# A two-layer early-fusion model on one core: image tokens built in two halves, and routed pages of 64 rows worked in pairs

## The chip, the core and the metric

The kernel runs on one core of one Trainium2 chip. The metric is the device time of one execution in microseconds (us). Before the change the median of three runs is 2499.37 us, with a lowest of 2489.65 and a highest of 2499.59. Everything is computed in float32.

## The reference

One function takes 128 images of 224 x 224, 32 text tokens of 64 numbers for each image, and the weights of two layers.

```
h = haar_tokens(x) @ W + b            # 7 wavelet maps, each resized to 8 x 8: 64 tokens of 64
h = concat([h, txt], axis=1)          # [128, 96, 64]: 64 image tokens, 32 text tokens
h = h + attention(layernorm(h))       # layer 0: gated attention, squared relu, rope
h = h + ffn(layernorm(h))             # layer 0: heads with 4 experts each
h = h + rwkv(layernorm(h))            # layer 1: the recurrence over 96 tokens, and its own ffn
h = h + moe(layernorm(h))             # layer 1: the part that the change touches most

def moe(x):                           # x: 128 * 96 = 12288 rows of 64
    logits = x @ Wr + br              # 64 experts
    top, idx = top_k(logits, 2);  gates = softmax(top)
    for e in range(64):
        y = relu(x @ W1[e] + b1[e]) @ W2[e] + b2[e]     # 64 -> 128 -> 64
        out += gate_of(e) * y
```

Each of the 12288 rows goes to two experts, so 24576 routed rows are computed.

## The kernel before

Each engine has one program, and semaphores join them. A helper, `grouped` (line 73), writes a software pipeline: it takes stages with a lag each, steps through iterations, and in step t calls each stage for iteration t minus its lag. So the order of the work on an engine is written by hand, as the order of the stages and their lags. `wait(engine, semaphore, n)` is a wait that is left out or trivial for the first iterations. An engine executes its program strictly in order; a wait holds up all that stands behind it on that engine.

*Tokenizer.* The 128 images are loaded in 32 groups (`NG`) of four by SyncE (`load_images`, line 419), through four buffers; the load of group g waits until TensorE has done group g - 4. For each group TensorE multiplies with the row filters (`image_rows`, 8 matmuls, line 476) and turns the result (`image_turn`, 2 transposes, line 484). ScalarE copies both out of PSUM (`keep_rows`, line 983, and `keep_turn`, line 990). Only when all 32 groups are done follow, once: the column products in two halves of 512 columns (line 495), two products for tables (lines 499 and 501; VectorE makes from them the selection matrices `gsel` and the rope tables, lines 1457 to 1472), the token products for each of the 8 token columns (line 509, 512 columns wide), copied with their bias by ScalarE (line 1000), and 16 turning steps of four transposes (line 518), which ScalarE copies into `H` (line 1004). SyncE loads the text rows after the images (line 424) and then writes zeros over `XD`, the DRAM buffer of routed rows, in 16 DMAs (line 430).

*The middle.* The attention, the first ffn, the recurrence and its ffn run from 144 to about 1740 us. The change leaves them alone.

*Routing.* 16 rounds (`NR`) of 8 batches. TensorE turns the normalized rows and computes the logits (`d_transpose`, `d_logits`), VectorE picks the best two experts and, with TensorE's counting products (`d_ranks`), a slot for each routed row (`d_places`, lines 1906 to 1946). The rows of an expert fill blocks of `SLOT` = 128 rows in `XD`, and a new block is opened where the last one is full; there are at most `NBLK` = 2 x 12288 / 128 + 64 = 256 blocks. `over` (line 1912) counts how many new blocks an expert opens in a round (at most 7), `tab1`/`tab2` (lines 1932 and 1933) mark which expert owns which block. GpSimd takes a power for the norm (`d_power`, line 1416), makes a label (line 1420) and scatters the rows by 12 indirect DMAs per round (`d_scatter`, line 1431), each row with its destination and its gate behind it (`ROW` = 66). At the end the table of the blocks' experts becomes `blku`, 256 words that ScalarE can read into a register (line 1955).

*Expert loop.* 64 iterations of `EB` = 4 blocks, 512 rows. For an iteration
- SyncE loads 4 blocks (`load_blocks`, line 437), one DMA, up to eight iterations ahead, waiting for `e_out` of eight iterations before;
- ScalarE picks the weights (`pick_weights`, lines 1301 and 1302): for each block it reads the expert's number from `blku` into a register (`value_load`) and copies 256 columns (W1 with its bias as a 65th row, W2, and b2) from `wall`, which holds all experts, into `wx`, a ring of four iterations that lies over `XR`;
- TensorE turns the rows (`e_transpose`, line 954), ScalarE copies them out (`e_rows`, line 1060) under a row of ones that two `memset` instructions have set (lines 1959 and 1960);
- TensorE computes the hidden values, 65 rows deep (`e_hidden`, line 963), VectorE takes the relu out of PSUM (`e_relu`, line 1965);
- TensorE computes the outputs (`e_output`, line 971), VectorE copies the destinations, adds b2 and multiplies by the gate (`e_out`, lines 1970, 1973, 1975);
- GpSimd stores the four blocks by four indirect DMAs to `YD` (`e_back`, line 1444), waiting for the stores of two iterations before.

After the loop SyncE loads `YD` back, two rows for each token, and VectorE adds them to `h`.

## Time and profile before

| what | value |
|---|---|
| runs shown, median (lowest to highest) | 2499.37 us (2489.65 to 2499.59) |
| the profiled execution: its own time | 2492.8 us |
| its span, first to last instruction | 2490.7 us |
| mean granted TensorE clock, share of full | 0.788 |
| busy: TensorE / VectorE / ScalarE / GpSimd | 1874.9 / 1614.3 / 1086.9 / 1086.6 us |
| chain that ended last, by engine | TensorE 31%, VectorE 23%, issue 18%, GpSimd 10%, unknown queue 9% |

A profile is one execution. PE is TensorE's matmul side, PEld its weight loads, DVE VectorE, ACT ScalarE, POOL GpSimd and SP SyncE. A busy time is the sum over an engine's instructions and says nothing of who waits for whom; for that one looks at what ended the idle time ahead of an instruction (the releaser). Register, branch, semaphore and DMA-issuing instructions aren't counted as busy, so an engine can be at work on them in a stretch that is shown as idle and named "issue". "remote" is written where the profile finds no releaser among the core's engines. Records of fp32 matmuls are several for each matmul of the program (x16 for the 8 of a group), so counts in the rows are records.

### The profile page before, as it was taken

The numbers are of one execution on the slowest core, as the hardware profiler recorded it, in microseconds if no ns is written. First come the engines' busy times: TensorE is split into PE (matmuls) and PEld (weight loads), VectorE is DVE, ScalarE is ACT, GpSimd is POOL, SyncE is SP. The second block draws the span as 40 slices with busy tenths as digits, with TensorE's granted clock in tenths as the row PEclk, the third lists the DMA queues.
The fourth block names the chain that finished last, engine by engine and source line by source line (L and its number), as shares of the span: only waits on it lengthen the run. The fifth ranks groups of instructions, "written<-read, shape, count | busy, mean of one in ns | idle before, by whom it ended". The sixth has DMA issues, their size and how long they took to land.

```text
span 2490.7 us, 52044 instructions
## 1 busy us (share of the span) xinstructions
PE 1874.9 (75%) x16279; PEld 1455.7 (58%) x16279; DVE 1614.3 (65%) x5056; ACT 1086.9 (44%) x3422; POOL 1086.6 (44%) x878
## 2 busy tenths in 40 slices
PE   5788887999999999999997477764333346766672
PEld 2257676777777777777775255553222236655562
DVE  0047773588888888888886699995888832222223
ACT  2277772344444444444443389883222123333330
POOL 0036660134434344434343322221888755655553
PEclk9989996899999999999997578796555555555555
DMA  9910000000000000000000000005100031111114
GB/s 283 287 58 0 0 0 1 1 2 2 2 0 0 0 0 0 0 0 0 0 0 1 0 1 1 1 0 172 37 23 22 23 94 41 42 39 37 40 35 164
DMA packets 85142, 87.76 MB, mean 35 GB/s; under 512 B 58560, under 2 KB 73024, under 8 KB 83776
## 3 DMA queue, kind: packets, MB, share of 16 engines
q1 hardware_dynamic: 70576, 68.63, 9.8%
q0 software_dynamic: 14336, 14.91, 1.8%
q10 hardware_dynamic: 144, 3.15, 0.3%
q8 instruction: 46, 0.75, 0.1%
q14 instruction: 40, 0.33, 0.0%
HBM read 56.82 MB, written 29.82 MB: 35 GB/s over the span
## 4 chain that ended last, share of the span: by engine, by line
PE 31%; DVE 23%; issue 18%; POOL 10%; another core or an unknown queue 9%; ACT 2%; DMA 1%; DVEq 1%; POOLq 0%; ACTq 0%; SPq 0%
POOL routed_rows L1431 5%; PE PS L674 5%; PE PS L641 3%; PE PS L708 3%; PE PS L689 3%; PE PS L971 2%; POOL rstd L1332 2%; DVE XR L1585 2%; DVE XR L1785 2%; DVE XR L1581 1%; PE PS L723 1%; PE PS L748 1%; DVE arena L1965 1%; PE PS L570 1%
## 5 line engine op out<-in xcount | busy, mean ns | idle before, releaser
L1444 POOL DMA_INDIRECT expert_rows<-arena x256 | 245.7, 960 | 193.2 <-DVE arena L1975 127.8
L1060 ACT ACTIVATE arena<-PS 128x384 f32<-128x384 f32 (+4 forms) x384 | 179.8, 486 | 306.1 <-remote 95.5
L1965 DVE TENSOR_SCALAR arena<-PS 128x512 f32<-128x512 f32 x64 | 44.3, 691 | 341.8 <-remote 216.4
L1581 DVE TENSOR_REDUCE XR<-PS 128x2 f32<-128x192 f32 (+2 forms) x768 | 173.8, 280 | 104.7 <-PE PS L674 104.7
L1431 POOL DMA_INDIRECT routed_rows<-XR,SLu x192 | 201.3, 1048 | 75.5 <-issue 70.4
L674 PE MATMUL PS<-arena 32*128 32x96 f32 (+2 forms) x3072 | 234.2, 285 | 0.0
L971 PE MATMUL PS<-XR,arena 128*128 128x64 f32 x512 | 126.0, 428 | 130.3 <-DVE arena L1965 130.2
L674 PEld LDWEIGHTS PS<-arena 32*128 32x128 f32 x3072 | 198.4, 192 | 20.6
L971 PEld LDWEIGHTS PS<-XR,arena 128*128 128x128 f32 x512 | 114.0, 328 | 157.2 <-DVE arena L1965 139.8
L1377 POOL TENSOR_TENSOR arena<-arena,mhalf 96x16 f32<-96x16 f32 x32 | 93.3, 2916 | 241.5 <-DVE arena L1627 241.5
L1096 ACT ACTIVATE XR<-PS 128x256 f32<-128x256 f32 x512 | 167.3, 380 | 67.1 <-PE PS L689 66.9
L1302 ACT ACTIVATE XR<-arena 128x256 f32 x256 | 106.6, 416 | 179.2 <-issue 113.4
L1060 ACT ACTIVATE XR<-PS 128x384 f32<-128x384 f32 (+1 forms) x160 | 83.5, 522 | 222.0 <-PE PS L708 167.6
L1585 DVE TENSOR_TENSOR XR<-PS,XR 128x192 f32<-128x192 f32 (+2 forms) x768 | 172.4, 278 | 0.0
L641 PE MATMUL PS<-arena,WP 128*128 128x192 f32 x640 | 151.4, 361 | 18.4 <-ACT arena L1060 17.9
L689 PE MATMUL PS<-WP,XR 128*128 128x128 f32 (+1 forms) x1024 | 163.6, 284 | 0.9 <-ACT XR L1096 0.9
L708 PE MATMUL PS<-XR,arena 96*32 96x128 f32 (+2 forms) x3072 | 148.7, 288 | 6.6 <-DVE arena L1600 5.0
L1367 POOL TENSOR_TENSOR XR<-arena 96x1024 f32<-96x1024 f32 x32 | 61.8, 1931 | 191.6 <-DVE arena L1617 191.6
L1332 POOL TENSOR_TENSOR rstd<-stat,mhalf 96x4 f32<-96x4 f32 x32 | 78.4, 2450 | 129.5 <-DVE stat L1492 129.5
L963 PE MATMUL PS<-arena,XR 65*128 65x128 f32 x512 | 129.4, 434 | 0.0
L641 PEld LDWEIGHTS PS<-arena,WP 128*128 128x128 f32 x640 | 105.5, 199 | 34.8 <-ACT arena L1060 19.7
L1351 POOL TENSOR_TENSOR rstd<-stat,mhalf 96x4 f32<-96x4 f32 x32 | 36.2, 1131 | 197.9 <-DVE stat L1554 184.3
(307 smaller groups left out, 4750.3 us busy)
## 6 DMA issues: line engine op xcount, KB each, us to landing
arena<-in_x_dram SPq DMA_DIRECT2D x32, 784.0 KB, 9.8
routed_rows<-zt SPq DMA_DIRECT2D x16, 528.0 KB, 6.0
arena<-routed_rows SPq DMA_DIRECT2D x64, 132.0 KB
arena<-in_t_experts_dram SPq DMA_DIRECT2D x8, 1024.0 KB, 12.5
expert_rows<-arena POOLq DMA_INDIRECT x256
WP<-in_t_pack_dram SPq DMA_DIRECT2D x1, 3425.0 KB, 20.3
mixed_rows<-Hb SPq DMA_DIRECT2D x4, 768.0 KB
routed_rows<-XR,SLu POOLq DMA_INDIRECT x192
```

The source lines that it names most:

```text
L641: mm = pe.matmul(o, w[:, par, :], sxF[:, u, :].rearrange("p (q t) -> p q t", q=2), start=True, stop=True)
L674: mm = pe.matmul(PS[:, S_ + i, S_AT[j]:S_AT[j] + QB * (j + 1)], qF[rows, u, 3 * b + j, :], kF[rows, u, keys], start=False, stop=True, skip ...
L689: mm = pe.transpose(PS[0:keys, T0_ + i, n * P:(n + 1) * P], Pe[:, p, i, n * P:n * P + keys], ident[:, :])
L708: mm = pe.matmul(PS[32 * n:32 * n + 32, O_, j * P:(j + 1) * P], Vx[rows, u, b * NH + n, :], PT[rows, b % 2, n, at:at + P], start=True, sto ...
L963: mm = pe.matmul(PS[:, 2 + u % 2, k * SLOT:(k + 1) * SLOT], wx[0:D + 1, u % WRING, k, 0:NHX], xT[:, u % 2, k * SLOT:(k + 1) * SLOT], start ...
L971: mm = pe.matmul(PS[:, 4 + u % 2, k * D:(k + 1) * D], hT[:, u % 2, k * SLOT:(k + 1) * SLOT], wx[:, u % WRING, k, NHX:NHX + D], start=True, ...
L1060: return act.activation(dst, src, ACT.Identity, **kw)
L1096: act.activation(PT[:, b % 2, 2 * p + i, :], bank(T0_ + i, P, 2 * P), ACT.Exp).then_inc(b_exp, 1)
L1431: pool.indirect_dma_start(XD, bass.IndirectOffsetOnAxis(SLu[:, u, k, b:b + 1], 0), XG[:, u, b, k, :], None).then_inc(scat[u], 16)
L1444: pool.indirect_dma_start(YD, bass.IndirectOffsetOnAxis(yi[:, u % 4, k:k + 1], 0), yb[:, u % 4, k, :], None).then_inc(e_st[u % 2], 16)
L1581: dve.tensor_reduce(negmax[:, p, j, :], PS[:, S_:S_ + 2, S_AT[j]:S_AT[j] + QB * (j + 1)], AX_X, ALU.max, negate=True).then_inc(b_max, 1)
L1585: dve.tensor_tensor(Pe[:, p, :, P_AT[j]:P_AT[j] + QB * (j + 1)], PS[:, S_:S_ + 2, S_AT[j]:S_AT[j] + QB * (j + 1)], negmax[:, p, j, :].unsq ...
```

## The change

*Tokenizer.* The 16 last groups of the loading loop are written out step by step (`part`), and in steps 17 to 25 TensorE and ScalarE also do, for the first 64 images, the column products (step 17), two token products each (18 to 21, now 256 columns wide, in banks 6 and 7) and two turns each (22 to 25). The second half of the images follows after the loop. The two table products come in the middle of the loop. In PSUM the turns move from banks 0 and 1 to 4 and 5.

*Pages.* `SLOT` becomes 64, so there are `NBLK` = 448 pages, in 56 iterations of `EB` = 8 pages, again 512 rows. `KB` = 4 is the number of 128-row pieces in which an iteration is loaded and stored: partitions 0 to 63 of a piece hold one page, 64 to 127 the next. The products of the two pages of a piece are written one after the other and lie on different halves of TensorE's array: rows for the hidden product (64 rows deep, results in two PSUM banks), columns for the output product, rows and columns for the transposes. The hidden bias is a column of the copied weights (257 columns, `WX`) and is added by VectorE ahead of the relu, which is an instruction of its own. The add of b2 is done for each half of the partitions. Each page has its own pick of weights, eight for an iteration, but one register load brings four page numbers, packed six bits each. `wx` needs more room, so its ring is shifted by two iterations and iteration 2 waits for the scatters. In the routing `over` counts up to 12 new pages, and the page tables have four columns of 128 pages for two.

```diff
 NX = 64
-SLOT = 128
+SLOT = 64
 NBLK = 2 * B * NTOK // SLOT + NX
 NHX = 128
-EB = 4
+KB = 4
+EB = KB * P // SLOT
+PC = -(-NBLK // P)
 CH = B // 4
 CHUNKS = 4
...
 RING = 8
 WRING = 4
-WX = NHX + 2 * D
+WX = NHX + 2 * D + 1
+BIAS = NHX + 2 * D
+PACK = 4
...
+            def image_cols(h):
+                pe.wait_ge(turn_kept, (h + 1) * (NG // 2))
+                wait(pe, tokT_kept, h * (B // 16))
...
+            def image_tokens(h, j):
+                pe.wait_ge(tok_kept, h * (GRID + 1) + 1 + max(j - 1, 0))
                 for par in range(2):
-                    mm = pe.matmul(PS[64 * par:64 * par + 64, 2 + j % 2, :], gsel[:, j, :], fv[:, par],
-                                   start=True, stop=True)
+                    mm = pe.matmul(PS[64 * par:64 * par + 64, 6 + j % 2, 0:256], gsel[:, j, :],
+                                   fv[:, par, h * (B // 4):(h + 1) * (B // 4)], start=True, stop=True)
                 mm.then_inc(tok_done, 1)
...
+            for t in range(NG // 2, NG + 1):
+                part(NG, t, (0, image_rows), unroll=4)
+                if t > NG // 2:
+                    part(NG, t, (1, image_turn), unroll=4)
+                at = t - NG // 2 - 1
+                if at == 0:
+                    image_cols(0)
+                    pe.wait_ge(gsel_done, GRID)
+                    pe.wait_ge(rope_set, 1)
+                elif 0 < at <= 4:
+                    for j in range(2 * at - 2, 2 * at):
+                        image_tokens(0, j)
+                elif 4 < at <= 8:
+                    for k in range(2 * at - 10, 2 * at - 8):
+                        image_tokens_turn(k)
+            image_cols(1)
+            for j in range(GRID):
+                image_tokens(1, j)
+            for k in range(B // 16, B // 8):
+                image_tokens_turn(k)
...
-                for k in range(EB):
-                    mm = pe.transpose(PS[0:D, u % 2, k * SLOT:(k + 1) * SLOT], xb[:, u, k, 0:D], ident[:, :])
+                for k in range(KB):
+                    for h in range(2):
+                        r = slice(h * SLOT, (h + 1) * SLOT)
+                        mm = pe.matmul(PS[r, u % 2, k * SLOT:(k + 1) * SLOT], xb[r, u, k, 0:D], ident[r, r], start=True, stop=True)
...
-                for k in range(EB):
-                    mm = pe.matmul(PS[:, 2 + u % 2, k * SLOT:(k + 1) * SLOT], wx[0:D + 1, u % WRING, k, 0:NHX],
-                                   xT[:, u % 2, k * SLOT:(k + 1) * SLOT], start=True, stop=True)
+                for k in range(KB):
+                    for h in range(2):
+                        r = slice(h * D, (h + 1) * D)
+                        mm = pe.matmul(PS[:, 2 + 4 * h + u % 2, k * SLOT:(k + 1) * SLOT], wx[r, (u + 2) % WRING, 2 * k + h, 0:NHX],
+                                       xT[r, u % 2, k * SLOT:(k + 1) * SLOT], start=True, stop=True)
...
-                for k in range(EB):
-                    mm = pe.matmul(PS[:, 4 + u % 2, k * D:(k + 1) * D], hT[:, u % 2, k * SLOT:(k + 1) * SLOT],
-                                   wx[:, u % WRING, k, NHX:NHX + D], start=True, stop=True)
+                for k in range(KB):
+                    for h in range(2):
+                        at = (h * KB + k) * SLOT
+                        mm = pe.matmul(PS[h * SLOT:(h + 1) * SLOT, 4 + u % 2, k * D:(k + 1) * D], hT[:, u % 2, at:at + SLOT],
+                                       wx[:, (u + 2) % WRING, 2 * k + h, NHX:NHX + D], start=True, stop=True)
...
+                if isinstance(g, int) and g == 2:
+                    for v in range(2):
+                        act.wait_ge(scat[v], 16 * NR * NV)
                 for k in range(EB):
-                    e = act.value_load(blku[0:1, ds(g * EB + k, 1)], min_val=0, max_val=NX - 1)
-                    a = act.activation(wx[:, u % WRING, k, :], wall[:, ds(e, 1), :].rearrange("p o w -> p (o w)"), ACT.Identity)
+                    if k % PACK == 0:
+                        four = act.value_load(blku[0:1, ds(g * (EB // PACK) + k // PACK, 1)], min_val=0, max_val=NX ** PACK - 1)
+                    e = (four >> (6 * (k % PACK))) & (NX - 1)
+                    a = act.activation(wx[:, (u + 2) % WRING, k, :], wall[:, ds(e, 1), :].rearrange("p o w -> p (o w)"), ACT.Identity)
                 a.then_inc(e_w, 1)
...
-                link(dve.tensor_tensor(over[:, :, :], fill[:, :].unsqueeze(2).broadcast_to([P, NX, 7]),
-                                       d_step[:, 2:9].unsqueeze(1).broadcast_to([P, NX, 7]), ALU.is_gt))
+                link(dve.tensor_tensor(over[:, :, :], fill[:, :].unsqueeze(2).broadcast_to([P, NX, OVER]),
+                                       d_step[:, PC:PC + OVER].unsqueeze(1).broadcast_to([P, NX, OVER]), ALU.is_gt))
...
+            page = PS[0:1, 6, 0:NBLK].rearrange("p (n j) -> p j n", j=PACK)
+            link(dve.tensor_copy(bpk[0:1, 1, :], page[:, 3, :]))
+            link(dve.scalar_tensor_tensor(bpk[0:1, 0, :], bpk[0:1, 1, :], float(NX), page[:, 2, :], ALU.mult, ALU.add))
+            link(dve.scalar_tensor_tensor(bpk[0:1, 1, :], bpk[0:1, 0, :], float(NX), page[:, 1, :], ALU.mult, ALU.add))
+            dve.scalar_tensor_tensor(blku[:, :], bpk[0:1, 1, :], float(NX), page[:, 0, :], ALU.mult, ALU.add).then_inc(d_blk, 1)
...
             def e_relu(g, u):
                 dve.wait_ge(e_up, g + 1)
                 wait(dve, e_down, g - 1)
-                dve.tensor_scalar(hT[:, u % 2, :], bank(2 + u % 2, P, EB * SLOT), 0.0, None, ALU.max).then_inc(e_h, 1)
+                link = Link(dve, d_cell, g, 1)
+                link.base += 4 * NR
+                link(dve.tensor_tensor(hT[:, u % 2, :].rearrange("p (h k r) -> p h k r", h=2, r=SLOT),
+                                       PS[:, 2 + u % 2:8:4, 0:KB * SLOT].rearrange("p h (k r) -> p h k r", r=SLOT),
+                                       wx[:, (u + 2) % WRING, :, BIAS].rearrange("p (k h) -> p h k", h=2).unsqueeze(3)
+                                       .broadcast_to([P, 2, KB, SLOT]), ALU.add))
+                dve.tensor_scalar(hT[:, u % 2, :], hT[:, u % 2, :], 0.0, None, ALU.max).then_inc(e_h, 1)
...
+                for h in range(2):
+                    r = slice(h * SLOT, (h + 1) * SLOT)
+                    add = dve.tensor_tensor(yb[r, u % 4, :, :], PS[r, 4 + u % 2, 0:KB * D].rearrange("p (k d) -> p k d", k=KB),
+                                            wx[r, (u + 2) % WRING, h::2, NHX + D:NHX + 2 * D], ALU.add)
+                    if h == 0:
+                        link.ahead(add)
+                    else:
+                        link(add)
```

## Rows read from the trace of the kernel before

**Rows 1.** groups by line, 0 to 146 us: count | busy, mean | idle

```profile
L476 PE MATMUL PS<-arena,WP 112*32 112x224 f32 x512 | 55.1, 580 | 37.7 <-DMA arena<-in_x_dram 37.7
```

**Rows 2.** timeline of TensorE: start, length, what, count [idle before <-releaser]

```profile
99.04 1.72 PE L476 MATMUL PS<-arena,WP 112*32 112x224 f32 x16 [0.42 <-DMA arena<-in_x_dram]
...
112.69 6.44 PE L495 MATMUL PS<-XR,WP 112*32 112x512 f32 x32 [0.53 <-ACT XR L990]
...
121.41 6.85 PE L509 MATMUL PS<-arena 128*64 128x512 f32 x20 [1.69 <-DVE arena L1470]
...
133.13 1.06 PE L518 MATMUL PS<-WP,arena 128*64 128x128 f32 x8 [1.28 <-ACT arena L1000]
```

**Rows 3.** timeline of ScalarE in the same stretch

```profile
124.80 8.27 ACT L1000 ACTIVATE arena<-PS,WP 128x512 f32<-128x512 f32 x7 [0.52 <-PE PS L509]
...
142.95 1.07 ACT L1004 ACTIVATE Hb<-PS 64x512 f32<-64x512 f32 x2 [0.23 <-PE PS L518]
```

**Rows 4.** timeline of GpSimd, a routing round

```profile
1799.31 1.69 POOL L1416 TENSOR_TENSOR arena<-arena,mhalf 96x8 f32<-96x8 f32 x1
...
1801.33 1.42 POOL L1431 DMA_INDIRECT routed_rows<-XR,SLu  x1 [0.17 <-POOL XR L1420]
...
1812.10 0.96 POOL L1431 DMA_INDIRECT routed_rows<-XR,SLu  x1 [0.32 <-issue]
...
1817.57 1.80 POOL L1416 TENSOR_TENSOR arena<-arena,mhalf 96x8 f32<-96x8 f32 x1
```

**Rows 5.** timeline of VectorE, the same round

```profile
1801.12 0.69 DVE L1878 TENSOR_TENSOR XR<-XR,arena 96x512 f32<-96x512 f32 x1 [1.86 <-POOL arena L1416]
...
1810.99 0.17 DVE L1945 CAST SLu<-arena 128x12 uint32<-128x12 f32 x1
```

**Rows 6.** windows: length, PE, PEld, DVE, ACT, POOL busy (x), PEclk, DMA share, GB/s

```profile
144.00:1740.00 1596.00, 1383.88 (x13898) 1097.01 (x13898) 1277.95 (x3972) 844.85 (x2713) 610.15 (x387) 0.90 0.02 7
2026.00:2464.00 438.00, 295.26 (x1280) 260.65 (x1280) 97.21 (x256) 142.27 (x316) 245.70 (x256) 0.50 0.15 39
```

**Rows 7.** timeline of VectorE in the expert loop, three relus in a row

```profile
2208.78 0.69 DVE L1965 TENSOR_SCALAR arena<-PS 128x512 f32<-128x512 f32 x1 [7.72 <-remote]
...
2213.34 0.69 DVE L1965 TENSOR_SCALAR arena<-PS 128x512 f32<-128x512 f32 x1 [3.02 <-issue]
...
2222.61 0.69 DVE L1965 TENSOR_SCALAR arena<-PS 128x512 f32<-128x512 f32 x1 [7.72 <-remote]
```

**Rows 8.** timeline of GpSimd there: a run's end, the next one's ends

```profile
2206.22 0.96 POOL L1444 DMA_INDIRECT expert_rows<-arena  x1 [0.30 <-issue]
2211.19 0.96 POOL L1444 DMA_INDIRECT expert_rows<-arena  x1 [4.01 <-DVE arena L1975]
...
2220.04 0.96 POOL L1444 DMA_INDIRECT expert_rows<-arena  x1 [0.30 <-issue]
```

**Rows 9.** timeline of TensorE there

```profile
2215.85 2.02 PE L963 MATMUL PS<-arena,XR 65*128 65x128 f32 x8
```

**Rows 10.** timeline of ScalarE there

```profile
2231.74 0.42 ACT L1302 ACTIVATE XR<-arena 128x256 f32 x1 [0.31 <-issue]
...
2241.71 0.42 ACT L1302 ACTIVATE XR<-arena 128x256 f32 x1 [3.01 <-issue]
```

**Rows 11.** groups by line and form, routing, 1740 to 2010 us

```profile
L1928 DVE TENSOR_TENSOR arena<-arena 128x768 f32<-128x768 f32 x15 | 14.4, 958 | 0.5
...
L1932 DVE TENSOR_TENSOR arena<-arena,WP 128x128 f32<-128x128 f32 x15 | 4.3, 284 | 0.0
```

**Rows 12.** the page's groups, the whole span

```profile
L674 PE MATMUL PS<-arena 32*128 32x96 f32 (+2 forms) x3072 | 234.2, 285 | 0.0
...
L689 PE MATMUL PS<-WP,XR 128*128 128x128 f32 (+1 forms) x1024 | 163.6, 284 | 0.9 <-ACT XR L1096 0.9
...
L708 PE MATMUL PS<-XR,arena 96*32 96x128 f32 (+2 forms) x3072 | 148.7, 288 | 6.6 <-DVE arena L1600 5.0
```

**Rows 13.** groups by line, expert loop, 2030 to 2460 us

```profile
L1973 DVE TENSOR_TENSOR arena<-PS,XR 128x256 f32<-128x256 f32 x64 | 26.7, 417 | 0.0
```

More of the change, by code:

```diff
@@ L155, in build @@
         H = Hb[0:NTOK, :]
-        XR = sb("XR", [P, B * D])
+        XRw = sb("XR", [P, WRING * EB * WX])
+        XR = XRw[:, 0:B * D]
         first_w, all_w = table[""]
@@ L1006, in _ @@
+            keep_cols(1)
+            for j in range(GRID):
+                keep_tokens(1, j)
+            for k in range(B // 16, B // 8):
+                keep_tokens_turn(k)
             T_, B_, U_, K_ = 0, 1, 3, 5
@@ L1442, in e_back @@
                 pool.sem_inc(go, 1)
-                for k in range(EB):
+                for k in range(KB):
                     pool.indirect_dma_start(YD, bass.IndirectOffsetOnAxis(yi[:, u % 4, k:k + 1], 0),
```

120 lines of the change are left out of this document (63 added, 57 removed).

## Prediction

> **What bounds the kernel now.** I read the windows by stage first, then the timelines of the three stretches that the diff touches, the tokenizer, the routing rounds and the expert loop, and last the rows that price single instructions. The long middle of the program is not edited, and I cost it at nothing.
>
> The tokenizer is bound twice. Until 112 us each group of four images waits for its DMA: TensorE's eight filter products take 1.72 us, and ahead of them it sits idle about 0.5 us per group, 37.7 us in all [rows 1, 2]. Then comes a serial tail: the column products start at 112.69, the token products at 121.41, the turning transposes at 133.13, and the last copy ends at 144.02 [rows 2, 3]. Nothing else of the program runs in these 31.3 us.
>
> The routing rounds are bound by POOL: from the `pow` at 1799.31 to the next at 1817.57 it issues 12 scatters without a pause. VectorE's chain in a round, from the norm at 1801.12 to the slots at 1811.16, is ready 0.94 us before the scatter that needs it starts at 1812.10 [rows 4, 5].
>
> The expert loop takes 438 us [rows 6]. TensorE's stages need 4.56 us an iteration (2208.78 to 2213.34), POOL's four stores 4 x 1.264 = 5.06 us (2211.19 to 2220.04 is seven steps), and yet two iterations take 13.83 us (2208.78 to 2222.61) [rows 7, 8]. The missing time has an odd shape. The hidden products end at 2217.87 [rows 9], but the relu that waits for them starts at 2222.61, which is 2.57 us after the start of POOL's last store of an unbroken run of eight (2220.04); the relu at 2208.78 is 2.56 us after that of the run before (2206.22). Early in a run nothing of that is seen: the relu at 2213.34 is in TensorE's own step. So a signal of TensorE that is due when POOL's run is 2.1 us old passes, and one due at 6.7 us is late until the run has landed. ScalarE is slowed too: it waits 3.01 us before its copy at 2241.71 [rows 10]. I call this a hold; why it is so the trace doesn't tell. A cycle of two iterations is then a sum: 2.41 us from relu to first store, 8.85 us to the start of the eighth, 2.57 us to the release, 13.83 us, and 32 cycles are 442.6 us against 438 measured, 4.6 us less for the shorter cycles at both ends.
>
> **The change, part by part.**
> *Tokenizer in halves.* Images 0 to 63 get their column products, tokens and turns inside the groups 17 to 25 of the loading loop, the other half afterwards. The tail that is left: half of the column products 3.2 us, their copy with its waits 1.0, eight token copies, eight turns. A token copy of 512 columns takes 1.18 us (8.27 us for seven); at 256 columns it lies between the half, 0.59, and the whole; I take 0.69, since a part of each instruction is fixed: 5.5 and 1.2 us to start up. The 16 turns take 10.9 us (133.13 to 144.02), so eight take 5.45. Sum 16.4 us, 14.9 saved. What is moved isn't free: 3.2 us of column products, 3.4 to 5.2 of token products and 4.4 of turns, 11 to 13 us, stand on TensorE's in-order queue in front of the next groups' products, against 15 remaining groups x 0.5 us = 8 us of idle time. TensorE then ends the loop 3 to 5 us late. ScalarE gets about 10 us of copies in nine groups in which it was mostly idle. The loads are issued when a group is done, four deep, so SP's loads slip with it but land before they are needed; the text load and the zero stores behind them on SP's queue end before they are used (the DMA share after 144 us is 0.02 [rows 6]). Gain 10 us (bounds 6 and 13). The tables' products and their selection by VectorE go to the middle of the loop, under the loads.
>
> *Routing rounds.* Four instructions per round grow from 128 to 256 elements and two from 448 to 768. From 0.958 us for 768 and 0.284 for 128 elements [rows 11], an element costs 1.05 ns: 2 x 0.34 + 3 x 0.135 = 1.08 us ahead of the slots and 0.135 behind them. The slack is 0.94 us, so POOL is held up 0.15 to 0.3 us a round: +4 us over 16 rounds. Bounds: 0 (slack) and 16 x 1.22 = 20 us. The few added instructions on the page table (two more products, three small VectorE steps, about 2 us) lie beside the last scatters, which end 14 us later. Fewer zero stores (14 for 16) change nothing, they run under the first stages.
>
> *Expert loop, count.* 448 pages of 64 rows in eights are 56 iterations, where 256 blocks of 128 in fours were 64. Rows per iteration stay 512, and so do SP's load and POOL's four stores. POOL alone: 283 us for 324.
>
> *Expert loop, TensorE.* Every stage issues 8 products in 16 records, for 4, 8 and 8 records before. Whether a pair on two halves of the array runs side by side this loop doesn't show, other rows do: the products on two row strips (L674) cost 234.2 us / 3072 = 76 ns a record and those on column strips (L708) 48 ns, where full-array products (L689) cost 160 ns [rows 12]. By that the hidden stage stays at about 1.8 us (loading 128 columns of weights sets it), transposes stay at 0.9, and the output stage falls from 1.8 to 0.9. Bounds for the iteration: 3.9 us with pairs side by side and the longer relu on the path, 7.0 us if pairs go one after the other. Neither bound is what a cycle waits for as long as the hold stands. The granted clock is 0.50, the lower of its two levels, all through the loop [rows 6]; I leave it there.
>
> *Expert loop, VectorE.* The bias row leaves the product, so the relu becomes an add from PSUM (0.69 us, as the relu now) and a max within SBUF, at 0.35 to 0.69 us, linked by a semaphore. The output add becomes two of 64 partitions; partitions don't shorten them, each costs the 0.417 us of today's [rows 13]. Both lie between the relu and the first store: 2.41 becomes 3.3 us (bounds 3.1 and 3.6). What is queued behind: the next relu, for which TensorE's output stage waits, still within POOL's 5.06 us.
>
> *Expert loop, ScalarE.* Eight copies of a page's weights at 0.42 us for four, but two register loads for four: one load holds four page numbers. Now a pick comes every 0.73 us (0.42 and 0.31 of issue [rows 10]). Without the load I take 0.4 to 0.5 us; with the row copy, now 256 columns, 4.5 us an iteration. That fits into 5.06, but in a hold ScalarE makes few picks, and outside it there are some 8.2 us a cycle (3.3 and, by an estimate between 2.1 and 6.7, 4.9 until the hold begins) for some 13 picks and two row copies: 13 x 0.5 + 1.2 = 7.7 us. Just enough; this is where the slower rival sits.
>
> Cycle after: 3.3 + 8.85 + 2.57 = 14.7 us, times 28 is 411.6, less the same 4.6: 407 us, 31 less than now.
>
> **Sum.** The profiled execution took 2492.8 us (span 2490.7 and 2.1 around it). -10 + 4 - 31 = -37: 2455.8. The median of the runs shown is 6.6 us above the profiled one, and I keep that distance: 2462 us.
>
> **Rivals.**
> A. *Three iterations in a run.* TensorE now comes round in about 3.9 us, so the hidden stage of a third iteration ends when POOL's run is 4.5 us old (2 x 3.9 - 3.3), between the ages of which today's rows show passing and late. Then a cycle is 3.3 + 11 x 1.264 + 2.57 = 19.8 us for three, 6.6 each: 56 x 6.6 - 5 = 364, 2419 us. For it: 4.5 is below 6.7. Against: TensorE sends 48 records an iteration for 20, and if the hold begins with a number of records and not with an age, it begins sooner. Two iterations pass in any case, because the second's hidden products end when the run is 0.6 us old.
> B. *No hold.* If it hangs on the register loads (halved) or on the blocks' form, POOL bounds: 56 x 5.06 + 13 us of filling = 296, 2351 us. Against: POOL's part, on which the release depends to 0.01 us, is unchanged.
> C. *Pairs don't pair.* 7.0 us of TensorE per iteration and POOL pausing between its stores: 56 x 7.0 and 5 of filling = 397, 2452 us. The change doesn't do what it says and the time is nearly that of the forecast.
> D. *The max slows POOL.* Beside a VectorE instruction with two SBUF inputs (0.69 us from 1801.12) a scatter took 1.42 us where 0.96 is usual [rows 4, 5]. Were each new max to cost a store 0.46 us, it would be 0.9 us a cycle, +25 us: 2487 us. For it: the max is the loop's first large instruction that has both its ends in SBUF. Against: most such instructions in the rounds leave the scatters at 0.96.
> The Trainium skill, SBUF — State Buffer, section "Who interferes with whom", says that `tensor_scalar` can enter a two-port mode in which it takes the port pair shared with GpSimd, whose descriptor writing is then locked out for the instruction. That would be D; the relu of today reads PSUM, and no row of this loop shows it.
> E. *The slower side: ScalarE's picks.* If a pick without its own load still costs the 0.73 us of today, because of the shift, the mask and the address, 13 picks and 1.2 us are 10.7 us against 8.2 free ones: +2.5 us a cycle, +70 us, 2532 us. It decides from 0.54 us a pick; slower than before it is from 0.64. For it: most of a pick's 0.73 us is sequencer work, and the 3 us waits in a hold. Against: the register load is the longest piece of it.
>
> **How the numbers follow.** Forecast 0.42, A 0.18, B 0.12, C 0.08, D 0.07, E 0.13. What this kernel's measurement tells from no change is 0.5%, 12.5 us. The forecast with its own bounds (2445 to 2485), A, B and C are faster: 0.78, of which I take 0.02 off for a forecast that falls short; D and that are the same: 0.10 with a shade of E; E is slower: 0.13, with that for a hold that begins sooner 0.14. The range 2370 to 2520 leaves out B's lower part and E's upper one.
>
> **What would show it.** Token turns of the second half end at 133 to 135 us: tokenizer right. Rounds of 18.4 us from `pow` to `pow` with POOL waiting for the slots: routing right. In the expert loop, relus in an alternation of about 4 and 10.7 us, each late one 2.57 us after the last of eight stores; 3.9, 3.9 and 12 us would be A; even steps of 5.06 B; even steps of 7 with pauses on POOL C. Products of a pair that start some ns apart against 100 or 200 ns decide C. Stores longer than 0.96 us would be D; relus or hidden products that wait for ScalarE's copies, E. I am wrong in the main if a cycle is not relu-to-store plus the run plus 2.57 us.

## The result and the profile after

The changed kernel takes 2484.07 us (median of 8 runs, 2482.36 to 2486.96), the kernel before 2498.0 in the same comparison (8 runs, 2489.65 to 2501.22): a ratio of 0.9934, interval 0.9914 to 0.9953, 16 us less by the ratio. Forecast were 37. The direction was right, the size was not: less than half of it came.

The profiled execution after has 2486.96 us and a span of 2485.1. Where the two traces differ, by landmarks that both have:

| stretch | before | after | difference | forecast |
|---|---|---|---|---|
| start to the end of the last token copy | 144.0 | 130.7 | -13.3 | -10 |
| to the first scatter | 1596.2 | 1597.8 | +1.6 | 0 |
| first to last scatter (starts) | 283.6 | 295.6 | +12.0 | +4 |
| last scatter to last store (starts) | 438.9 | 433.2 | -5.7 | -31 |
| to the end of the span | 27.9 | 27.8 | -0.2 | 0 |

The traces are 5.6 us apart and the medians 14, because the profiled execution of before is one of its shorter ones and that of after its longest. Over all traces of this document, two stretches spread. The last token copy ends at 124.2 to 136.6 us in the eleven kernels with the new tokenizer (130.2 in the mean; their last image load was issued at 90.8 to 103.3 us) and at 138.8 to 144.0 in the three with the old one (141.2). From there to the first scatter twelve traces take 1593.0 to 1598.2 us and two, x6 and x9, 1606.7. So the first row of the table overstates the tokenizer by some 2 us; the mean difference is 11. The rounds repeat within 2 us and the loop within some 4 where the code is the same.

*Tokenizer.* Timeline of TensorE after: first and last of the half that moved into the loop, the eight filter products of two groups (L480), then the tail (columns as in [rows 2]); below it a group's filter products before.

```profile
69.11 2.79 PE L501 MATMUL PS<-XR,WP 112*32 112x512 f32 x16
...
91.35 0.96 PE L480 MATMUL PS<-arena,WP 112*32 112x224 f32 x16 [0.84 <-DMA arena<-in_x_dram]
...
92.51 1.04 PE L519 MATMUL PS<-WP,arena 128*64 128x128 f32 x8
...
103.66 1.72 PE L480 MATMUL PS<-arena,WP 112*32 112x224 f32 x16 [0.75 <-DMA arena<-in_x_dram]
...
112.69 3.67 PE L501 MATMUL PS<-XR,WP 112*32 112x512 f32 x16 [0.53 <-ACT XR L1021]
117.10 5.50 PE L510 MATMUL PS<-arena 128*64 128x256 f32 x24 [0.74 <-ACT arena L1025]
```
```profile
90.62 1.72 PE L476 MATMUL PS<-arena,WP 112*32 112x224 f32 x16 [0.60 <-DMA arena<-in_x_dram]
```

The column products of the tail start at 112.69, where they started before [rows 2] (to the hundredth by chance: 107.6 to 118.6 in the other kernels with this tokenizer). The moved products take 11.3 us, and yet the loop is no longer. What paid for most of them isn't idle time: it stands ahead of the filter products of the last 15 groups with 10.3 us, for 10.1 before. The filter products themselves became shorter. From 71.7 to 95.4 us a group's eight take 0.94 to 0.97 us for 1.72, and its turns 0.43 for 0.68; over the tokenizer that is 47.6 us for 55.1, and 19.1 for 21.5 of turns, 9.9 us together. The granted clock of after is 1.00 from 70.9 us, in the middle of the moved column products, to 98.2, and 0.50 from there to 112, where a group takes 1.72 us again. The trace of before has no granted clock ahead of 118 us; all its 32 groups take 1.72, as at 0.50. All eleven traces with the new tokenizer have 8 to 11 groups under 1.1 us in this stretch, the three with the old one none.

*Routing.* The group of the scatters before and after (count | busy, mean ns | idle ahead of them), then POOL's timeline in one round after. POOL is GpSimd.

```profile
L1431 POOL DMA_INDIRECT routed_rows<-XR,SLu x192 | 201.3, 1048 | 75.5 <-issue 70.4 <-DVE SLu L1945 2.8 <-POOL XR L1420 2.2
```
```profile
L1488 POOL DMA_INDIRECT routed_rows<-XR,SLu x192 | 208.9, 1088 | 81.1 <-issue 77.8 <-POOL XR L1477 2.2 <-DVE SLu L2002 0.9
```
```profile
1804.16 0.95 POOL L1488 DMA_INDIRECT routed_rows<-XR,SLu  x1 [0.90 <-issue]
...
1813.09 1.25 POOL L1488 DMA_INDIRECT routed_rows<-XR,SLu  x1 [0.30 <-issue]
```

The 12 us have two parts: the scatters themselves last 7.6 us more in sum, and between the first and the last of them POOL waits 4.5 us more (0.90 ahead of the scatter at 1804.16, the first of its round that needs the slots, where 0.30 is usual). The row's 5.6 us contain 1.1 from ahead of the very first scatter.

*Expert loop.* Timelines after of VectorE (relus), POOL (first and last store of a run) and TensorE. A run is a series of POOL's stores without a pause, 1.26 us from start to start; its age counts from its first start.

```profile
2067.78 0.69 DVE L2024 TENSOR_TENSOR arena<-PS,XR 128x512 f32<-128x512 f32 x1 [8.36 <-remote]
2068.50 0.43 DVE L2028 TENSOR_SCALAR arena<-arena 128x512 f32<-128x512 f32 x1
...
2072.06 0.69 DVE L2024 TENSOR_TENSOR arena<-PS,XR 128x512 f32<-128x512 f32 x1 [1.81 <-PE PS L992]
...
2082.98 0.69 DVE L2024 TENSOR_TENSOR arena<-PS,XR 128x512 f32<-128x512 f32 x1 [8.45 <-remote]
```
```profile
2071.06 0.96 POOL L1501 DMA_INDIRECT expert_rows<-arena  x1 [5.26 <-DVE arena L2044]
...
2079.95 0.96 POOL L1501 DMA_INDIRECT expert_rows<-arena  x1 [0.30 <-issue]
```
```profile
2070.04 1.97 PE L992 MATMUL PS<-arena,XR 64*128 64x64 f32 x16
2071.94 1.12 PE L981 MATMUL PS<-WP,arena 64*64 64x64 f32 x16
2073.34 1.12 PE L1002 MATMUL PS<-XR,arena 128*64 128x64 f32 x16 [0.28 <-DVE arena L2028]
2074.40 1.54 PE L992 MATMUL PS<-arena,XR 64*128 64x64 f32 x10
2076.85 0.26 PE L992 MATMUL PS<-arena,XR 64*128 64x64 f32 x1 [0.91 <-issue]
2077.56 0.26 PE L992 MATMUL PS<-arena,XR 64*128 64x64 f32 x1 [0.45 <-issue]
```

TensorE's own step is 4.28 us (2067.78 to 2072.06), but a cycle of two iterations is 15.20 here. From relu to first store 3.28 us, from there to the eighth store 8.89, from that to the next late relu 3.03. And now the hold, as the prediction calls the delay of signals during a run of stores, is visible on TensorE itself: from 2076 on its products come one or two at a time, 0.7 us apart.

### The profile page after: what moved, and what is told of

The parts are those of the page before. It is cut to its first block, busy times and chain, and to the rows that moved or that the text cites. A ratio compares the mean times of both kernels' runs of the same rounds, so it can differ in the third digit from the quotient of the medians.

```text
span 2485.1 us, 55409 instructions
## 1 busy us (share of the span) xinstructions
PE 1843.3 (74%) x17723; PEld 1432.8 (58%) x17723; DVE 1667.6 (67%) x5137; ACT 1113.8 (45%) x3614; POOL 1062.9 (43%) x846
## 4 chain that ended last, share of the span: by engine, by line
PE 34%; DVE 22%; issue 18%; POOL 14%; DMA 4%; another core or an unknown queue 4%; ACT 3%; DVEq 1%; POOLq 0%; SPq 0%; ACTq 0%
POOL routed_rows L1488 8%; PE PS L698 5%; PE PS L992 5%; DMA arena<-in_x_dram 4%; PE PS L665 3%; PE PS L732 3%; POOL rstd L1389 3%; PE PS L713 3%; PE PS L1002 2%; DVE XR L1642 2%; DVE XR L1842 2%; DVE XR L1638 1%; PE PS L747 1%; PE PS L772 1%
## 5 line engine op out<-in xcount | busy, mean ns | idle before, releaser
L1112 ACT ACTIVATE arena<-PS 128x384 f32<-128x384 f32 (+2 forms) x376 | 162.7, 451 | 342.6 <-remote 147.6
L1501 POOL DMA_INDIRECT expert_rows<-arena x224 | 215.3, 961 | 217.9 <-DVE arena L2044 155.8
L1488 POOL DMA_INDIRECT routed_rows<-XR,SLu x192 | 208.9, 1088 | 81.1 <-issue 77.8
L2024 DVE TENSOR_TENSOR arena<-PS,XR 128x512 f32<-128x512 f32 x56 | 38.7, 692 | 295.9 <-PE PS L992 199.5
L992 PE MATMUL PS<-arena,XR 64*128 64x64 f32 x896 | 148.8, 410 | 89.8 <-issue 89.0
L1359 ACT ACTIVATE XR<-arena 128x257 f32 x448 | 153.3, 407 | 111.3 <-issue 90.7
L992 PEld LDWEIGHTS PS<-arena,XR 64*128 64x128 f32 x896 | 128.1, 316 | 102.0 <-issue 94.6
L713 PEld LDWEIGHTS PS<-WP,XR 128*128 128x128 f32 (+1 forms) x1024 | 115.2, 130 | 9.3 <-DVE XR L1642 1.4
```

What stands on the lines that cost most here:

```text
L713: mm = pe.transpose(PS[0:keys, T0_ + i, n * P:(n + 1) * P], Pe[:, p, i, n * P:n * P + keys], ident[:, :])
L992: mm = pe.matmul(PS[:, 2 + 4 * h + u % 2, k * SLOT:(k + 1) * SLOT], wx[r, (u + 2) % WRING, 2 * k + h, 0:NHX], xT[r, u % 2, k * SLOT:(k + 1 ...
L1112: return act.activation(dst, src, ACT.Identity, **kw)
L1359: a = act.activation(wx[:, (u + 2) % WRING, k, :], wall[:, ds(e, 1), :].rearrange("p o w -> p (o w)"), ACT.Identity)
L1488: pool.indirect_dma_start(XD, bass.IndirectOffsetOnAxis(SLu[:, u, k, b:b + 1], 0), XG[:, u, b, k, :], None).then_inc(scat[u], 16)
L1501: pool.indirect_dma_start(YD, bass.IndirectOffsetOnAxis(yi[:, u % 4, k:k + 1], 0), yb[:, u % 4, k, :], None).then_inc(e_st[u % 2], 16)
```

## The experiments

Ratios are to the kernel before, timed on the same chip. The changed kernel was not timed again; comparisons with it go by the quotient of the ratios. That quotient has an error of its own. For each of the nine runs on the changed kernel it comes out 4 to 15 us less favourable than what the traces show in rounds and loop, always to the same side, while for x1, x2 and x11, which differ from the kernel before, ratio and trace agree within 4 us. The kernel before took 2498.0 us in the comparison with the changed kernel and 2487.7 to 2488.5 in the three later ones. So the 16 us of the result may be some 10 too many; why, is not known. Below, both figures are given where they differ.

**x1 and x2: each part alone.** The tokenizer's part of the diff on the kernel before, and the rest of the diff on it.

> The kernel before with the tokenizer's part of the change alone. Additive theory (the parts don't touch each other): the last token copy ends at 130.7 as in the changed kernel instead of 144.0, the first scatter comes 12 us earlier, rounds (18.1 us) and expert loop (438.9 us from last scatter to last store) stay, so 12 to 13 us less, ratio 0.995. Rival (the early start is given back later, by clock or code loading): less than 6 us are left at the end.

> The kernel before with the pages of 64 rows alone, tokenizer as before. Additive theory: routing rounds of 19.0 us for 18.1 cost 12 us, the expert loop (last scatter to last store 433.2 for 438.9) gives 5.7, so 4 to 7 us slower than before, ratio 1.002. Rival (the rounds are longer because the tokenizer's change moved something): rounds of 18.1 to 18.4 us, and then 2 to 6 us faster than before.

Measured: x1 0.9962 (0.9943 to 0.9980), 9 us less; x2 1.0005 (0.9988 to 1.0022), nothing. In the traces x1 has 282.7 us from first to last scatter and x2 295.8, and last scatter to last store takes 442.5 and 429.1. So by stretches the parts add up, and the longer rounds belong to the pages, which as a whole bring nothing that can be measured. By the ratios the two give 8 us where the whole gave 16, with 4 or 5 us of uncertainty on each of the three; the traces are nearer to the 8.

**x3: POOL waits for the last four stores to land.**

```diff
-                wait(pool, e_st[u % 2], (g - u % 2) * 32)
+                wait(pool, e_st[(u + 1) % 2], (g + u % 2) * 32)
```

> The changed kernel, but POOL waits before the four stores of an iteration until the four of the iteration before have landed (it waited for those of two before). Theory of the hold by age (TensorE's signals are held from about 5 us after the start of an unbroken run of stores until the run has landed): runs of four are 3.8 us long and land at 5.8, so hardly anything is held, an iteration takes 6.3 to 6.8 us evenly instead of 7.49, and the kernel gets 38 to 60 us faster than the changed one, though POOL waits more. Rival 1 (the hold has nothing to do with the length of a run, it comes with TensorE's and ScalarE's own instructions): the wait only adds to the cycle, 8 us or more an iteration, 30 us slower or more. Rival 2 (POOL's pause costs what the hold gives back): within 10 us of the changed kernel.

Measured: 0.9861 (0.9833 to 0.9890), 18 us less than the changed kernel by the quotient and 33 by the traces. The theory gave 38 to 60. Timelines of POOL and of VectorE's relus in x3:

```profile
2343.10 0.96 POOL L1501 DMA_INDIRECT expert_rows<-arena  x1 [0.30 <-issue]
2346.03 0.96 POOL L1501 DMA_INDIRECT expert_rows<-arena  x1 [1.97 <-issue]
...
2349.83 0.96 POOL L1501 DMA_INDIRECT expert_rows<-arena  x1 [0.30 <-issue]
```
```profile
2344.88 0.69 DVE L2024 TENSOR_TENSOR arena<-PS,XR 128x512 f32<-128x512 f32 x1 [4.18 <-remote]
...
2351.78 0.69 DVE L2024 TENSOR_TENSOR arena<-PS,XR 128x512 f32<-128x512 f32 x1 [4.43 <-remote]
```

Steps of mostly 6.6 to 7.0 us, 6.46 in the mean, from last scatter to last store 399.9 us for 433.2. A wait that makes POOL pause more makes the loop faster. But the onset at 5 us of age fell: the hidden products of this iteration end at 2349.1, when the run is 3.1 us old, and their relu comes at 2351.78, 1.95 us after the run's last store has started.

**x4: 448 elements for 768 in the routing.** `OVER` 7 for 12.

> The changed kernel, but a round can open at most 7 new pages for an expert instead of 12, so the two VectorE instructions on that table have 448 elements again (0.62 for 0.96 us each); the page table keeps its four columns. Where an expert got more than 448 rows in a round, rows would be misplaced. Chain theory (POOL waits for the slots, 0.37 us a round more than before): VectorE is ready 0.66 us earlier, that wait goes, 18.5 to 18.6 us a round, 6 us faster. Collision theory (half of the 12 us comes from scatters that meet certain VectorE instructions and take 1.1 to 1.6 us instead of 0.96): the meetings shift, and the excess over 0.96 us, 25.5 us in all against 17.9 before, falls by some us more, to 8 to 12 us faster in all.

Measured: 0.9921 (0.9895 to 0.9947), not distinguishable from the changed kernel. Its trace is clearer: first to last scatter 288.6 us for 295.6, scatters busy 204.7 us for 208.9. Both theories hold a part: 4.2 of the 7.0 us are shorter scatters, 2.8 less waiting.

**x5: POOL waits for three of the last four.** The last store of an iteration has a semaphore of its own.

```diff
-                wait(pool, e_st[u % 2], (g - u % 2) * 32)
+                wait(pool, e_sl[u % 2], (g - u % 2) * 8)
+                wait(pool, e_st[(u + 1) % 2], (g + u % 2) * 24)
...
```

> The changed kernel, but POOL waits before the stores of an iteration until the first three stores of the iteration before have landed (x3 waited for all four). Such a wait ends 2.93 us after the start of the store it waits for (2343.10 to 2346.03 in x3), so POOL steps at 2.53 + 2.93 = 5.5 us an iteration, and its run is never landed as a whole. Release by a short pause: even iterations of 5.5 to 6 us, 50 to 60 us faster than x3. Release only when everything has landed (the theory): TensorE's signals stay held while POOL goes on, POOL runs dry as in the changed kernel, 7 to 7.6 us an iteration in the mean, no faster than the changed kernel by over 10 us.

Measured: 0.9963 (0.9942 to 0.9984), slower than x3. The alternation of 4.28 and 10.7 us is back, with eight stores in a row, although POOL pauses some 0.8 us in place of 0.30 between the fourth and the fifth. So a pause of 0.8 us, with three stores landed, doesn't end the hold; one of 1.97 us, with all four landed (x3), does. Whether it is the landing of everything or the length of the pause that counts, these two runs don't separate.

**x6 and x11: plain DMAs for the indirect stores.** In the changed kernel and in the kernel before.

```diff
-                    pool.indirect_dma_start(YD, bass.IndirectOffsetOnAxis(yi[:, u % 4, k:k + 1], 0),
-                                            yb[:, u % 4, k, :], None).then_inc(e_st[u % 2], 16)
+                    pool.dma_start(YD[ds(g * (EB * SLOT) + k * P, P)], yb[:, u % 4, k, :]).then_inc(e_st[u % 2], 16)
...
```

> The changed kernel, but the four indirect stores of an iteration are four plain DMAs of POOL to consecutive rows (the rows don't get to their tokens' places; the bytes are the same). If the hold comes from indirect stores, whose start costs POOL 1.26 us each, the loop runs at TensorE's 4.3 us an iteration: 56 x 4.3 + 19 = 260 us for 430, 150 to 175 us faster. If it comes from the bytes or the number of DMAs on the queue, the alternation 4.28 and 10.8 us stays, within 20 us of the changed kernel.

> The kernel before with plain DMAs in place of the indirect stores, as x6 is to the changed one (rows not in their tokens' places). Without the hold the loop runs at TensorE's own 4.57 us: 64 x 4.57 + 19 = 311 us for 439, some 128 us faster than before. Then the pages, at 56 x 4.30, are worth 50 us of loop where nothing is held, and 6 where it is: the gain of the change went into the hold. Rival (the pages gain nothing by themselves): 64 steps of 4.0 us or less.

Measured: x6 0.9263 (0.9225 to 0.9301), x11 0.9465 (0.9443 to 0.9486). Relus of x6 and of x11, and POOL of x6:

```profile
2149.63 0.69 DVE L2023 TENSOR_TENSOR arena<-PS,XR 128x512 f32<-128x512 f32 x1 [1.81 <-PE PS L992]
2153.91 0.69 DVE L2023 TENSOR_TENSOR arena<-PS,XR 128x512 f32<-128x512 f32 x1 [1.81 <-PE PS L992]
```
```profile
2144.13 0.69 DVE L1964 TENSOR_SCALAR arena<-PS 128x512 f32<-128x512 f32 x1 [3.02 <-PE PS L963]
2148.70 0.69 DVE L1964 TENSOR_SCALAR arena<-PS 128x512 f32<-128x512 f32 x1 [3.01 <-PE PS L963]
```
```profile
2148.58 2.33 POOL L1501 DMA_DIRECT2D expert_rows<-arena  x4 [1.90 <-DVE arena L2043]
```

Even steps of 4.28 and 4.57 us, which is what TensorE needs. From last scatter to last store 253.2 and 304.3 us: without the hold the pages are worth 51 us of loop, with it 6. So the indirect stores are the cause of the hold. Which property of theirs it is stays open: with plain DMAs POOL is also at work for only 2.33 us an iteration, in place of 5.06, and so pauses in each; the rows written are consecutive as well.

**x7, x8: fewer products.** Each of TensorE's stages in the loop does one, or two, of its four pairs (`range(KQ)` for `range(KB)`).

> The changed kernel, but each of TensorE's three stages in the expert loop does only one of its four pairs, so 12 records of matmuls an iteration for 48 (three quarters of the products are left out; POOL, VectorE, ScalarE and the DMAs do all of theirs). Leaky theory (during POOL's run TensorE's instructions can be reported only slowly, about one record in 0.36 us as between 2076.85 and 2082 in the changed kernel, which is 14 in an iteration of POOL's 5.06 us, behind a store for some 20; the signal of an instruction comes only when it is reported): 12 records fit, no hold, POOL sets even steps of 5.06 us, 110 to 140 us faster than the changed kernel. Age theory (the hold begins a few us after the start of a run whatever TensorE does): relus still late until the run has landed, cycles of two iterations near 15 us or shorter by the 3 us that TensorE saves, at most 60 us faster.

> The same with two of the four pairs, 24 records an iteration (half of the products are left out). Leaky theory: 24 come and 14 go in 5.06 us, so some 10 more are in store after each iteration, and a store of about 20 is full after two iterations: runs of 12 or 16 stores for 8, 6.3 to 7 us an iteration in the mean, 25 to 65 us faster than the changed kernel. Age theory: runs of 8 as before, at most 40 us faster from TensorE's shorter stages.

Measured: x7 0.9899 (0.9859 to 0.9939), x8 0.9828 (0.9787 to 0.9869), 9 and 26 us less than the changed kernel (23 and 31 by the traces); 7.10 and 6.96 us an iteration for 7.48. Runs have mostly 12 stores in x7, and mostly 8, some 4 or 12, in x8, with late relus at their end. The leaky theory gave even steps for x7 and runs of 12 or 16 for x8, and fell. The age theory's bounds on the time hold in both, but the runs of 12 in x7 speak against an onset by age alone. Who is late in x7 is another engine. ScalarE, then TensorE:

```profile
2097.97 0.42 ACT L1360 ACTIVATE XR<-arena 128x257 f32 x1 [3.87 <-issue]
2100.05 0.42 ACT L1360 ACTIVATE XR<-arena 128x257 f32 x1 [1.66 <-issue]
2101.52 0.42 ACT L1360 ACTIVATE XR<-arena 128x257 f32 x1 [1.05 <-issue]
...
2109.41 0.72 ACT L1360 ACTIVATE XR<-arena 128x257 f32 x2 [0.99 <-issue]
```
```profile
2110.55 0.69 PE L993 MATMUL PS<-arena,XR 64*128 64x64 f32 x4 [13.88 <-ACT arena L1113]
```

Eight picks take 12.2 us late in a run (2097.97 to 2110.13), where at the start of one, in the changed kernel at 2071.15, four of them take 1.34, and the hidden products wait for them.

**x9, x10: ScalarE without register work.** Weights of fixed pages, copied without load, shift and address; in x10 also only one of four pairs of products.

```diff
-                    e = (four >> (6 * (k % PACK))) & (NX - 1)
-                    a = act.activation(wx[:, (u + 2) % WRING, k, :], wall[:, ds(e, 1), :].rearrange("p o w -> p (o w)"), ACT.Identity)
+                    a = act.activation(wx[:, (u + 2) % WRING, k, :], wall[:, 8 * u + k, :], ACT.Identity)
```

> The changed kernel, but ScalarE copies weights of fixed pages, without register loads, shifts and addresses (the experts are wrong, the copies are as many and as large); TensorE does all its products. Theory after x7 (during a run of indirect stores every engine's instructions get through only slowly, some tenths of a us each after the first dozens, and the loop waits for whichever engine has most of them): TensorE's 48 records alone hold the loop, so the cycle stays at 14.5 to 15.1 us for two iterations, within 15 us of the changed kernel. Rival (it is the register instructions of ScalarE that hold everything): steps of 5.06 us, 110 to 140 us faster.

> Fixed pages as in x9 and one of four pairs of TensorE's products as in x7. Theory of the choke: with both engines short of instructions nothing is held, POOL sets even steps of 5.06 us, the loop takes 56 x 5.06 + 19 = 302 us for 433, 120 to 135 us faster than the changed kernel. Rival (the hold comes by age, whatever the engines do): cycles of 7 us an iteration as in x7, within 40 us of the changed kernel.

Measured: x9 0.9947 (0.9921 to 0.9973), cycles of 14.9 us as forecast; x10 0.9704 (0.9676 to 0.9731), 57 us less than the changed kernel by the quotient and 72 by the traces, neither the 120 to 135 of the choke nor under 40. Relus of x10, in a run of 20 stores that begins at 2153.32:

```profile
2150.04 0.69 DVE L2022 TENSOR_TENSOR arena<-PS,XR 128x512 f32<-128x512 f32 x1 [9.56 <-remote]
...
2159.13 0.69 DVE L2022 TENSOR_TENSOR arena<-PS,XR 128x512 f32<-128x512 f32 x1 [1.63 <-remote]
...
2169.03 0.69 DVE L2022 TENSOR_TENSOR arena<-PS,XR 128x512 f32<-128x512 f32 x1 [7.43 <-remote]
```

Here signals get through in the middle of a run, 1.7 and 7.6 us after the hidden products end (2159.13 and 2169.03, while POOL's stores go on until 2177.87). So the hold isn't a closed door but a slow one, and it is felt by how much an engine has to bring through it. It never vanished while POOL stored indirectly.

**x12: a version.** x3's wait, and the number of new pages from two instructions of 64 elements.

```diff
-                link(dve.tensor_tensor(over[:, :, :], fill[:, :].unsqueeze(2).broadcast_to([P, NX, OVER]),
-                                       d_step[:, PC:PC + OVER].unsqueeze(1).broadcast_to([P, NX, OVER]), ALU.is_gt))
+                link(dve.tensor_scalar(over[:, :], fill[:, :], 1.0 / SLOT, 31.5 / SLOT, ALU.mult, ALU.add))
...
-                link(dve.tensor_reduce(nb[:, 0, 1:NX + 1], over[:, :, :], AX_X, ALU.add))
+                link(dve.tensor_scalar(nb[:, 0, 1:NX + 1], over[:, :], 12582912.0, -12582912.0, ALU.add, ALU.add))
```

> A version: the changed kernel with POOL's wait of x3, and in the routing the number of new pages by two small instructions of 64 elements, (n + 31.5) / 64 rounded with the help of 12582912, in place of the comparison with 12 steps and its sum (0.96 and 0.95 us, 768 elements). VectorE's chain in a round gets 1.5 us shorter: POOL no longer waits for the slots and sets rounds of 17.6 to 18.4 us, 283 us in all for 295.6. With the 33 us of x3's loop and 12 of the rounds, 40 to 50 us faster than the changed kernel, ratio to before 0.977. If the collisions of scatters with VectorE's instructions only move, the rounds stay at 18.7 and it is 5 us better than x3.

Measured: 2437.27 us, ratio 0.9799 (0.9780 to 0.9818), 50 us less than the kernel before, and 34 less than the changed kernel by the quotient, 45 by the traces (forecast 40 to 50, ratio 0.977). First to last scatter takes 284.1 us; in the row of its scatters both parts of the 12 us are gone again:

```profile
L1488 POOL DMA_INDIRECT routed_rows<-XR,SLu x192 | 202.6, 1055 | 74.4 <-issue 70.2 <-POOL XR L1477 2.2 <-DVE SLu L2001 1.8
```

## Why the prediction was wrong in size

*Tokenizer: right in size, one step by luck.* The tail takes 18.0 us (112.69 to 130.74) for 16.4 forecast, and TensorE leaves the loop on time instead of 3 to 5 us late. The moved work was sized rightly (11.3 us for 11 to 13), but the idle time that was to take it in stayed unused; the filter products and turns that got 9.9 us shorter paid for it, and the prediction had no such term. The 11 us saved in the mean of the traces (13.3 in this pair) agree with the 10 forecast for that reason.

*Routing: the larger part of the term was missing, and the slack was misread.* The durations came out as worked out (0.96 for the two of 768 elements, 0.42 for those of 256), and POOL's waiting too, 0.30 us a round (4.5 / 15) for 0.15 to 0.3, but that by luck. The 0.94 us between slots and scatter that it took for slack are almost all the way of the signal: in all 16 rounds of all traces the scatter starts no sooner than 0.84 us after the cast that writes the slots has ended, and after, with POOL idle ahead of it (0.46 to 1.11 us), it starts 0.84 to 1.14 us after. So some 0.1 of the 0.94 was slack. The 1.08 us of longer chain cost only 0.30 a round, because most rounds before had more slack than the one read (the scatter came 1.06 to 1.48 us after the cast), and because POOL's own scatters got longer by 0.5 us a round at the same time. What the step left out are the scatters that get longer, 7.6 us. They can be read one by one. Timelines of VectorE after, then of VectorE and POOL before, around the same scatter of a round (after it is the one at 1813.09, above).

```profile
1812.55 0.96 DVE L1969 TENSOR_TENSOR over<-arena,WP 128x768 f32<-128x768 f32 x1
```
```profile
1802.51 0.63 DVE L1912 TENSOR_TENSOR arena<-arena,WP 128x448 f32<-128x448 f32 x1
```
```profile
1803.05 0.96 POOL L1431 DMA_INDIRECT routed_rows<-XR,SLu  x1 [0.30 <-issue]
```

Before, the comparison had 0.09 us left when the scatter started at 1803.05; after, it has 0.42 left at 1813.09, and the scatter takes 1.25 us for 0.96. Over all 192 scatters of each trace, those over 0.1 us longer than the usual 0.96 are those that find a `tensor_tensor` with both inputs in SBUF under way at their start, and they are longer by about what that has left, less 0.12 us (less 0.03 beside the norm's product, L1878 and L1935): 39 of the 40 lengthened scatters before and 72 of 73 after start beside such an instruction. The reverse has exceptions: six scatters before with 0.26 to 0.72 us left are not lengthened, and all six start within 0.05 us of the VectorE instruction's own start. The prediction had seen one such scatter (its rival D) and set it aside, because "most such instructions in the rounds leave the scatters at 0.96". But most such instructions meet no scatter at its start; of the 45 scatters before that found more than 0.22 us of one left, 39 were longer. The 15 that start beside L1981, which has one input in PSUM and 0.35 us left, are not lengthened at all.

The Trainium skill, SBUF — State Buffer, section "Who interferes with whom", says that a DVE instruction with two SBUF inputs contends with a GpSimd instruction that reads SBUF. The trace agrees for these scatters. For the new max in the loop, for which the prediction cites the same section beside its rival D, it shows next to nothing: the store at 2072.32, beside the max of 2072.78, took 1.01 us for 0.96.

*Expert loop: the step that failed is the last one, "times 28 is 411.6, less the same 4.6".* The cycle itself was read rightly: relu to store 3.28 us (forecast 3.3), stores 8.89 (8.85); the release comes mostly 2.9 to 3.1 us after the last store's start (2.57). But 13.83 us was the commonest cycle before, not the mean. From first to last relu the loop before took 419.0 us, 6.65 an iteration, 13.3 a cycle. Of the 16.6 us that 31.5 cycles of 13.83 are too long, four cycles of 12.4 make up 5.7, and these are gone after; most of the rest are shorter steps at the two ends. In those four the hold ended before the run had landed: the relu came 0.6 to 1.2 us after the last store's start, not 2.57, so that the release was not fixed "to 0.01 us", as two relus had suggested. One of them, in timelines of VectorE and POOL before:

```profile
2093.03 0.69 DVE L1965 TENSOR_SCALAR arena<-PS 128x512 f32<-128x512 f32 x1 [3.01 <-issue]
...
2100.86 0.69 DVE L1965 TENSOR_SCALAR arena<-PS 128x512 f32<-128x512 f32 x1 [6.28 <-remote]
```
```profile
2099.76 0.96 POOL L1444 DMA_INDIRECT expert_rows<-arena  x1 [0.30 <-issue]
```

The rest of the 438.9 us, 19.9, is filling and emptying, which doesn't shrink with the count. The "4.6 less at both ends" stood in for both and hid them. With the forecast's own 14.7: 27.5 cycles and 19.9 are 424, -15 for -31. The other 9 us: 14.95 a cycle for 14.7 (7 us), and filling and emptying of 22.1 (2 us).

*The rivals.* A, three iterations in a run: no; the second signal after the start of a run is held too. In x7 and x10 runs became longer with fewer instructions, as the doubt noted at A expected. B, no hold: not here; x6 shows what it would have been worth. C: no, the pairs go side by side: the two products of a pair start 7 to 14 ns apart in the trace's records, the next pair 0.21 us later in the hidden stage and 0.11 in the two others. D: no, 961 ns a store for 960. E: no in its form, four picks take 1.54 us from start to start at the start of a run (2071.15 to 2072.69), 0.39 each; in x7 its mechanism is what bounds.

*What stays open* is by which path POOL's indirect stores slow the others, and what sets the onset. Relus due at ages of 3.6 and 4.0 us passed before (2231.90 and 2423.05), one due at 2.1 is late after (2261.30), and in x3 they are late at 3.1; neither an age nor a number of instructions fits all kernels. That the recording of the profile itself takes part can't be excluded: no run is without it.

## What to carry to other kernels

When a loop alternates between two step lengths, take its mean from first to last over all iterations, separate filling and emptying, and multiply only what scales with the count. Before making a loop's stages shorter, replace what is suspected of the wait by something cheaper that leaves a piece of its work out (here plain DMAs, whose rows don't get to their places; 167 us by the ratios): one run tells whether the stages or the wait are worth the work. Lengthening a VectorE `tensor_tensor` with both inputs in SBUF is paid on POOL as well, if it is then under way when POOL starts a scatter. And a small difference between two comparisons is to be checked against the stretches of the traces, before it is put down to the change.

## What the runs showed of the hardware

While POOL issues indirect stores back to back, instructions and signals of TensorE and ScalarE come late, most of them only when the last store has landed (picks 1.4 to 2.8 us from start to start in x7 for 0.39; TensorE 0.7 us per product or pair), some in the middle of a run (x10). With plain DMAs of the same bytes from POOL nothing is late (x6, x11). Waiting for landings before the next four stores, 2.93 us from the last store's start to the next store, is cheaper than the hold: 6.5 us an iteration in the mean for 7.5. An indirect store occupies POOL for 1.26 us from start to start, a plain DMA of the same 128 rows for about 0.6 (four in 2.33 us). A scatter that starts beside a `tensor_tensor` with two SBUF inputs lasts longer by what that has left, less 0.03 to 0.12 us; beside one with an input in PSUM it doesn't (15 of 15). A scatter starts no sooner than 0.84 us after the VectorE cast that writes its slots has ended. Eight filter products take 0.96 us at a granted clock of 1.00 and 1.72 at 0.50. In the eleven kernels that have the moved products between them they ran at the shorter length for 8 to 11 groups of the second half of the loading loop, in the three without them never.
